# The order of the first four row-major score groups of a head pair, in a one-core attention and feed-forward layer

## The chip, the cores and the metric

One NeuronCore of a Trainium2 chip runs the whole layer. The metric is the device time of one execution in microseconds; the engines are PE (TensorE), DVE (VectorE), ACT (ScalarE), POOL (GpSimd) and SP (SyncE, which issues the transfers).

## The reference

The input x is (8, 1024, 256) in float32. With 16 heads of 16 query and key dimensions and 64 value dimensions:

```python
Q = _split_heads(x, H)
K = _split_heads(x @ Wk + bk, H)
V = _split_heads(x @ Wv + bv, H)
scores = jnp.einsum('bhqd,bhkd->bhqk', Q, K) + mask      # causal
attn = jax.nn.softmax(scores, axis=-1)
o = jnp.einsum('bhqk,bhkd->bhqd', attn, V)
y = x + jax.nn.gelu(o, approximate=False) @ Wf + bf
x = _layernorm(x + y)
x = _layernorm(x + ffn(x))          # silu(x wg) * (x wu), times wd
```

## The kernel before

The program has three parts. A short first part projects keys and values of two units of 512 tokens. The middle part, `attend`, runs 69 steps over 64 pairs of heads (8 batches, 8 pairs each) and takes most of the time. The last part, `finish`, does the output product, the layer norms and the feed-forward product per unit of 512 tokens.

**What a step does.** The scores of a pair are computed twice. In step r, the *row-major* scores of pair r are formed (queries on the partitions), and DVE takes the maximum of each row from them. Two steps later, in step r + 2, the *transposed* scores of the same pair are formed (keys on the partitions) with the maxima already subtracted inside the product, ACT writes their exponentials to `weights`, POOL masks the diagonal blocks and adds the blocks up for the denominators, and PE multiplies them with the values (`weigh`). So in a step, row-major work of pair r stands beside transposed work of pair r - 2. Both come in twelve groups of two heads: s0 to s11 for the row-major groups (listed in `GS` as query tile and key half), t0 to t11 for the transposed ones (`GT`).

**The ring.** Scores go through three two-bank PSUM buffers (`ring`, line 704 is the matmul helper) in the fixed order t0 s0 t1 | s1 t2 s2 | t3 s3 t4 | s4 t5 s5 | t6 s6 t7 | s7 t8 s8 | t9 s9 t10 | s10 t11 s11. Each bar ends one of eight blocks of the step. A buffer comes free for its third successor: PE forms t(j + 2) only when DVE has taken the maximum of s(j) (so t2 waits for s0, t3 for s1, t4 for s2, t5 for s3), and s(j + 1) only when ACT has made the exponential of t(j). PE works strictly in program order, so a group that waits holds back everything behind it, the products with the values too: weigh of t9 and t10 of the pair before follow t1, that of t11 follows s2, those of t0 and t1 follow t4, each at its block's end.

**The maxima on DVE.** A row-major group is 128 queries by up to 512 keys for each of two heads. `top` handles three kinds: a *full* first half (query tiles 4 to 7, key half 0) is one reduction of 128x1024 into `part_max` (line 1109); a group with a causal diagonal is two custom instructions, one for each head, of 128, 256, 384 or 512 columns with the mask added (line 1117, each followed by the read of its accumulator); a second half (key half 1) does the same and takes the stored part maximum in.

**What else DVE does in a step.** In block 1, after s1 and s2, it transposes the shift parts (line 1129). In every fourth step (r divisible by 4, up to 52) it converts the next input unit: the high part after s3 (line 1071), the low part in block 4. In steps 5, 9, ... 53 it adds the bias to keys and splits them *ahead of s0* (lines 1082 and 1086), because the key projection of the step before has ended by then. In blocks 4 and 5 it begins the sum of weights (lines 1138, 1143).

**Projections beside the steps.** Up to step 55, PE also runs two or three projection products (six matmuls of 512 columns each) in a step, one of them at the end of block 1 (behind s2 and the product of t11), the others at the ends of blocks 6 and 7. From step 57 on there are none.

**The loop.** Steps 0 to 11 are written out, steps 12 to 51 are ten rounds of a loop whose body is four steps, and steps 52 to 68 are written out again. So steps 16, 20, ... 48 begin right behind a branch on each engine. The loop's top is at line 76, and the step's shift transposition begins with a register instruction of line 1124.

Of the kernel before, what the change touches and what calls it, by code (L numbers as in the profile page):

```python
# [51 lines left out]
SROWS = 48  # L52
SHROWS = 2
GT = tuple((0, u) for u in range(4)) + tuple((1, u) for u in range(8))
GS = ((0, 0), (4, 0), (5, 0), (2, 0), (6, 0), (7, 0), (1, 0), (4, 1), (5, 1), (3, 0), (6, 1), (7, 1))
NS = 12
NBURST = 8
RINGP = 3
# [24 lines left out]
def settle(eng, passed):  # L83


    eng.sem_inc(passed, 1)
# [7 lines left out]
def build(nc, xT, x, Wk, bk, Wv, bv, Wf, bf, wg, wu, wd, out):  # L94
# [26 lines left out]
    with ExitStack() as ctx:  # L121
# [580 lines left out]
        def _(pe):  # L702
# [54 lines left out]
            def score(j, r, n, it):  # L757

                q, k = Q[r % RING], K[r % RING]
                u, kc = GS[j]  # L760
                w = min(BANK, P * (u + 1) - BANK * kc)
# [285 lines left out]
        def _(dve):  # L1047
# [55 lines left out]
            def top(j, r, n):  # L1103

                u, kc = GS[j]
                w = min(BANK, P * (u + 1) - BANK * kc)
# [5 lines left out]
                if kc == 1:  # L1112

                    dve.wait_ge(s_max, NS * n + GS.index((u, 0)) + 1)
                    settle(dve, s_passed["dve"])
# [200 lines left out]
```

## Time and profile before

| what | value |
|---|---|
| median of 3 runs | 1959.52 us (1958.96 to 1960.97) |
| profiled execution | 1962.14 us, its span 1960.4 us |
| busy share of the span | PE 95%, DVE 73%, POOL 59%, ACT 53% |
| mean granted TensorE clock | 0.976 of full speed |
| steps 36, 37, 38, 39 (start of t0 to start of the next t0) | 23.90, 20.37, 21.46, 19.94 us |
| step 59 and step 60 (no projections) | 19.22 and 20.83 us |

The span is the time from the first to the last instruction of the profiled execution, which is 1.7 us less than its own device time. A step is the unit to think in: 64 of them with row-major work, some 20 us each. A matmul's recorded end is modelled, so the busy share of PE says little about spare time; the starts of successive groups say more.

### The profile page before, as it was taken

How to read it: one execution, taken by the hardware profiler on the slowest of the kernel's cores; microseconds unless marked ns; L12 is line 12 of the kernel's file. 1: busy time of each engine (PE TensorE's matmuls, PEld its weight loads, DVE VectorE, ACT ScalarE, POOL GpSimd, SP SyncE). 2: the span in 40 equal slices, each digit the busy share in tenths (PEclk: the TensorE clock that was granted, in tenths of full speed). 3: DMA queues.
4: the chain of work that ended last, by engine and by line, in shares of the span. 5: the costliest groups of instructions: out<-in, count | busy, mean ns of one | idle time of the engine just before them, and what ended most of it. 6: DMA issues, size and time to landing. Idle time of an engine off the chain costs nothing. (4 is left out here: it accounts for less than half of the span.)

```text
span 1960.4 us, 38648 instructions
## 1 busy us (share of the span) xinstructions
PE 1855.1 (95%) x10304; PEld 961.9 (49%) x10304; DVE 1424.2 (73%) x3469; ACT 1039.1 (53%) x1523; POOL 1158.1 (59%) x1328
## 2 busy tenths in 40 slices
PE   6799999999999999999999999989898999999996
PEld 5344444444444444444444444333255777767773
DVE  3877877777786777778677777767537787887874
ACT  2155555555555555555555556555554564555643
POOL 2187777777768777776877786887832122221222
PEclk9699999999999999999999999999899999999998
DMA  8955556455565545555454664456157667566610
GB/s 267 252 152 158 166 138 185 132 175 158 143 181 132 173 132 174 159 144 182 132 170 131 178 166 142 116 156 151 60 133 181 182 158 190 167 160 180 163 55 22
DMA packets 261008, 303.55 MB, mean 155 GB/s; under 512 B 28048, under 2 KB 177680, under 8 KB 260880
## 3 DMA queue, kind: packets, MB, share of 16 engines
q1 hardware_dynamic: 260880, 302.19, 55.6%
q14 instruction: 90, 0.74, 0.1%
q8 instruction: 38, 0.62, 0.1%
HBM read 174.20 MB, written 127.93 MB: 154 GB/s over the span
## 5 line engine op out<-in xcount | busy, mean ns | idle before, releaser
L964 ACT ACTIVATE weights<-ring 128x1024 f32<-128x1024 f32 (+3 forms) x768 | 599.2, 810 | 332.8 <-PE ring L704 328.1
L672 POOL TENSOR_TENSOR weight_sum<-weight_sum,weights 128x512 f32<-128x512 f32 (+3 forms) x448 | 682.0, 1522 | 9.8
L704 PE MATMUL o_acc<-weights,v_pair 128*64 128x512 f32 (+3 forms) x3072 | 620.1, 510 | 10.8 <-POOL weights L636 6.0
L1109 DVE TENSOR_REDUCE part_max<-ring 128x2 f32<-128x1024 f32 x256 | 301.3, 1218 | 129.4 <-PE ring L704 129.4
L636 POOL TENSOR_SCALAR_AFFINE_SELECT weights<-weights 128x256 f32<-128x256 f32 x512 | 217.6, 430 | 298.1 <-ACT weights L964 297.4
L695 POOL TENSOR_TENSOR h_lo<-hidden,h_hi 128x512 f16<-128x512 f32 x96 | 114.2, 1191 | 391.2 <-ACT h_hi L933 391.2
L704 PE MATMUL ring<-q_stack,k_stack 50*128 50x512 f32 (+3 forms) x1536 | 308.4, 407 | 37.6 <-DVE rowmax L1117 23.0
L1117 DVE CUSTOM_DVE_ANT_0 scrap<-ring,causal 128x128 bf16<-128x128 f32 (+3 forms) x512 | 229.5, 486 | 135.4 <-PE ring L704 132.0
L704 PE MATMUL ring<-k_stack,q_stack 48*128 48x512 f32 (+3 forms) x1536 | 304.2, 399 | 18.0 <-DMA k_stack<-k_rows 8.9
L704 PEld LDWEIGHTS o_acc<-weights,v_pair 128*64 128x64 f32 x3072 | 174.4, 137 | 234.1 <-issue 198.8
L1117 DVE CUSTOM_DVE_ANT_0 scrap<-ring,causal,part_max 128x128 bf16<-128x128 f32 (+3 forms) x512 | 251.1, 546 | 47.6 <-PE ring L704 47.2
L704 PEld LDWEIGHTS ring<-q_stack,k_stack 50*128 50x128 f32 x1536 | 144.9, 186 | 250.9 <-DVE rowmax L1117 114.5
L704 PEld LDWEIGHTS ring<-k_stack,q_stack 48*128 48x128 f32 x1536 | 147.2, 189 | 198.6 <-ACT weights L964 143.0
L704 PE MATMUL ring<-wf_sb,g 128*128 128x256 f32 x1024 | 230.5, 380 | 1.4 <-DVE y_pre L1206 0.8
L704 PEld LDWEIGHTS ring<-wf_sb,g 128*128 128x128 f32 x1024 | 191.4, 190 | 31.6 <-issue 2.2
L933 ACT ACTIVATE v_unit<-o_acc 128x512 f32<-128x512 f32 x112 | 67.0, 599 | 255.2 <-PE o_acc L704 255.2
L1159 DVE TENSOR_TENSOR g<-g,den_wide 128x512 f32<-128x512 f32 x128 | 147.8, 1180 | 8.8 <-DMA g<-o_heads 6.8
L672 POOL TENSOR_TENSOR weight_sum<-weights 128x768 f32<-128x768 f32 x64 | 116.6, 1821 | 0.0
L704 PE MATMUL o_acc<-wv_hi,x_hi 128*128 128x512 f32 x224 | 101.3, 452 | 0.0
L1138 DVE TENSOR_TENSOR weight_sum<-weights 128x1024 f32<-128x1024 f32 x64 | 78.1, 1220 | 18.2 <-PE o_acc L704 18.2
L704 PE MATMUL o_acc<-wv_lo,x_hi 128*128 128x512 f32 x224 | 89.3, 399 | 0.0
L704 PE MATMUL o_acc<-wv_hi,x_lo 128*128 128x512 f32 x224 | 88.7, 396 | 0.0
(105 smaller groups left out, 2057.5 us busy)
## 6 DMA issues: line engine op xcount, KB each, us to landing
v_pairs<-v_unit SPq DMA_DIRECT2D x64, 512.0 KB, 3.5
v_pair<-v_pairs SPq DMA_DIRECT2D x64, 512.0 KB, 5.3
o_heads<-o_pair SPq DMA_DIRECT2D x64, 512.0 KB, 3.5
g<-o_heads SPq DMA_DIRECT2D x16, 2048.0 KB, 8.1
den_wide<-reciprocals SPq DMA_DIRECT2D x32, 1024.0 KB, 13.3
q_stack<-q_rows SPq DMA_DIRECT2D x128, 192.0 KB, 3.7
k_stack<-k_rows SPq DMA_DIRECT2D x128, 192.0 KB, 4.3
q_rows<-x_hi SPq DMA_DIRECT2D x32, 512.0 KB, 3.6
```

What stands on the lines that cost most here:

```text
L636: pool.affine_select(out=diag, in_=diag, compare_op=ALU.is_ge, fill=0.0, base=0, pattern=[[0, 2], [1, P]], channel_multiplier=-1).then_inc ...
L672: pool.tensor_tensor(dst, other, W[t][:, :, :], ALU.add).then_inc(s_add, 1)
L695: pool.tensor_tensor(h_lo[:, f], h32[f % 2][:], h_hi[:, f], ALU.subtract).then_inc(s_hl, 1)
L704: return nc.tensor.matmul(o, l, r, start=start, stop=stop)
L933: return nc.scalar.activation(o, i, ACT.Copy)
L964: nc.scalar.activation(W[t][:, :, :], bank_of("t", t)[:, :, 0:width_of(t)], ACT.Exp).then_inc(s_w, 1)
L1109: v.tensor_reduce(part[r % 2][:, u - 4, :], bank_of("s", j)[:, :, 0:w], AX.X, ALU.max).then_inc(s_max, 1)
L1117: e = v.tensor_tensor_reduce(out=scrap[j % 2][h][:, 0:w], in0=bank_of("s", j)[:, h, 0:w], in1=causal[:, BANK - w:BANK], scale=1.0, scalar= ...
L1138: v.tensor_tensor(acc1[:], W[4][:], W[5][:], ALU.add).then_inc(s_add1, 1)
L1159: v.tensor_tensor(g[r % 2][:, c], g[r % 2][:, c], dn[r % 2][:, c], ALU.mult).then_inc(s_gn, 1)
```

## The change

The table `GS` gives the order in which the row-major groups of a pair are formed by PE and reduced by DVE. The first four entries change places; the other eight stay.

```diff
-GS = ((0, 0), (4, 0), (5, 0), (2, 0), (6, 0), (7, 0), (1, 0), (4, 1), (5, 1), (3, 0), (6, 1), (7, 1))
+GS = ((4, 0), (0, 0), (2, 0), (5, 0), (6, 0), (7, 0), (1, 0), (4, 1), (5, 1), (3, 0), (6, 1), (7, 1))
```

| group | before | after |
|---|---|---|
| s0 | diagonal block of 128 columns | full, 512 columns |
| s1 | full, 512 columns | diagonal block of 128 columns |
| s2 | full, 512 columns | diagonal block of 384 columns |
| s3 | diagonal block of 384 columns | full, 512 columns |

Each group of two heads keeps its work on every engine. The full groups of query tiles 4 and 5 still come ahead of the second halves (s7 and s8) that need them.

## Rows read from the trace of the kernel before

**Rows 1.** The page's head, whole execution

```profile
span 1960.4 us, 38648 instructions
```

**Rows 2.** Groups by line and shape, DVE, 400 to 1240 us: busy, mean, idle

```profile
L1109 DVE TENSOR_REDUCE part_max<-ring 128x2 f32<-128x1024 f32 x159 | 187.2, 1218 | 69.9 <-PE ring L704 69.9
...
L1117 DVE CUSTOM_DVE_ANT_0 scrap<-ring,causal 128x384 bf16<-128x384 f32 x80 | 41.4, 555 | 18.9 <-PE ring L704 18.4
...
L1117 DVE CUSTOM_DVE_ANT_0 scrap<-ring,causal 128x128 bf16<-128x128 f32 x80 | 20.0, 288 | 41.6 <-PE ring L704 39.0 <-issue 2.6
```

**Rows 3.** Timeline of step 37, DVE: start, duration, line, operation, idle before

```profile
831.12 0.75 DVE L1086 SCALAR_TENSOR_TENSOR k_lo<-o_acc,bk_sb,k_hi 128x512 fp32r<-128x512 f32 x1
831.78 0.28 DVE L1117 CUSTOM_DVE_ANT_0 scrap<-ring,causal 128x128 bf16<-128x128 f32 x1
...
832.61 2.36 DVE L1109 TENSOR_REDUCE part_max<-ring 128x2 f32<-128x1024 f32 x2 [0.33 <-PE ring L704]
```

**Rows 4.** Timeline of step 37, PE: t2, then the products of t0 and t1

```profile
832.41 0.32 PE L704 MATMUL ring<-q_stack,k_stack 50*128 50x256 f32 x2
...
835.77 1.72 PE L704 MATMUL o_acc<-weights,v_pair 128*64 128x512 f32 x8
```

**Rows 5.** Timeline of step 38, PE (s0, t2)

```profile
850.40 0.23 PE L704 MATMUL ring<-k_stack,q_stack 48*128 48x128 f32 x2
...
852.34 0.28 PE L704 MATMUL ring<-q_stack,k_stack 50*128 50x256 f32 x2
```

**Rows 6.** Timeline of step 38, DVE (s0)

```profile
850.82 0.29 DVE L1117 CUSTOM_DVE_ANT_0 scrap<-ring,causal 128x128 bf16<-128x128 f32 x1 [0.94 <-PE ring L704]
```

**Rows 7.** Timeline of step 36, behind the loop's branch, DVE

```profile
808.36 0.29 DVE L1117 CUSTOM_DVE_ANT_0 scrap<-ring,causal 128x128 bf16<-128x128 f32 x1 [2.77 <-PE ring L704]
...
812.67 0.21 DVE L1129 STREAM_TRANSPOSE shiftT<-shift_parts 128x32 f32<-128x32 f32 x1 [1.53 <-issue]
...
813.90 1.77 DVE L1071 CAST x_hi<-xt 128x1024 fp32r<-128x1024 f32 x1
815.59 2.34 DVE L1109 TENSOR_REDUCE part_max<-ring 128x2 f32<-128x1024 f32 x2
```

**Rows 8.** Timeline of step 36, PE: t2, t4, t6

```profile
808.93 0.39 PE L704 MATMUL ring<-q_stack,k_stack 50*128 50x256 f32 x2 [0.69 <-DVE rowmax L1117]
...
811.83 0.40 PE L704 MATMUL ring<-q_stack,k_stack 50*128 50x512 f32 x2
...
816.86 0.50 PE L704 MATMUL ring<-q_stack,k_stack 50*128 50x512 f32 x2 [0.16 <-DVE part_max L1109]
```

**Rows 9.** Line 1124 in step 36: DVE's queue (DVEq), register instruction

```profile
L1124 DVEq FUSED_REGOPS  x1: 64/64/64, 812.4 to 812.4; - x1
```

**Rows 10.** DMA queues, 810.3 to 811.3 us: packets, MB, share of 16 engines

```profile
q14 instruction: 1, 0.01, 1.9%
```

**Rows 11.** Timeline of step 61 (no projections), DVE, PE and POOL

```profile
1333.43 0.44 PE L704 MATMUL ring<-q_stack,k_stack 50*128 50x384 f32 x2 [0.69 <-DVE rowmax L1117]
...
1335.58 2.35 DVE L1109 TENSOR_REDUCE part_max<-ring 128x2 f32<-128x1024 f32 x2 [1.78 <-PE ring L704]
...
1336.86 0.33 PE L704 MATMUL ring<-q_stack,k_stack 50*128 50x128 f32 x2 [0.60 <-DVE part_max L1109]
...
1337.34 0.41 POOL L636 TENSOR_SCALAR_AFFINE_SELECT weights<-weights 128x256 f32<-128x256 f32 x1
...
1337.99 0.50 PE L704 MATMUL ring<-q_stack,k_stack 50*128 50x512 f32 x2 [0.58 <-DVE part_max L1109]
...
1338.39 0.77 POOL L636 TENSOR_SCALAR_AFFINE_SELECT weights<-weights 128x256 f32<-128x256 f32 x2
...
1338.42 3.25 PE L704 MATMUL o_acc<-weights,v_pair 128*64 128x512 f32 x8
```

**Rows 12.** Windows of steps 59 and 61: length, busy by engine, PEclk, DMA

```profile
1298.00:1302.00 4.00, 4.00 (x28) 1.47 (x28) 2.36 (x6) 2.54 (x3) 4.00 (x6) 1.00 0.42 92
...
1338.00:1342.00 4.00, 4.00 (x12) 1.31 (x14) 0.98 (x5) 1.51 (x2) 4.00 (x6) 0.57 1.07 217
```

## The prediction

> **What bounds the kernel now.** I read the page first, then DVE's groups by shape, then the timelines of single steps on PE and DVE, since the change moves nothing but the order inside a step. The sum is made against the profiled execution, 1962.14 us with a span of 1960.4 us [rows 1]; that is 2.6 us above the median of the runs, so I add the change of the span to 1959.5 us. Within 0.2% (3.9 us) a measurement of this kernel can't tell a change from none.
>
> No engine has less work or more after the change. What can move is who waits. The price list on DVE: a full group is one reduction of 1.22 us; a diagonal group of 384 columns is two instructions of 0.56 us, one of 128 columns two of 0.29 us [rows 2]. What counts for PE is the time from DVE's start on a group to the matmul that it lets go. For the 128-column group that is 0.57 us (s0 at 808.36, t2 at 808.93), for a full one 1.27 us (s4 at 815.59, t6 at 816.86) [rows 7, 8]. So with s0 full, t2 can come 0.70 us later after the same start of DVE. With s1 at 128 columns, t3 gets free earlier by the same amount, with s2 at 384 columns t4 a little, and t5 waits for a full s3. PE is in program order: whatever t2 loses, the products and projections behind it lose too. The reader is to see in each step whether t2 or t3 and t4 are the ones that wait.
>
> **The five kinds of steps.** Counts come from the loops and conditions in the code.
>
> *Ordinary steps* (29, like step 38). PE forms s0 at 850.40, and DVE starts on it at 850.82, idle until then [rows 5, 6]. A full s0 has 384 more columns, at 2.4 GHz 0.16 us, so DVE would start at 850.98 and let t2 go at 852.25. PE arrives at t2 at 852.34 [rows 5], and that arrival does not move, since s0's extra 0.16 us is what s1 saves. Nothing lost, nothing won; the margin is 0.1 us, so I keep ±0.05 us a step, ±1.5 us in all. The later t1 leaves ACT's exponential on time, because ACT is still on t0's.
>
> *Steps with a key split ahead of s0* (13: steps 5, 9, ... 53). In step 37 DVE comes to s0 only at 831.78, directly behind the key split that starts at 831.12 [rows 3]. Now t2 could go at 831.78 + 0.57 = 832.35 and does go at 832.41 [rows 4]: on the edge. With a full s0 it goes at 831.78 + 1.27 = 833.05, 0.64 us later. Until the products of t0 and t1 at 835.77 [rows 4] PE has 3.36 us filled with s2, a product, a projection and t3, s3, t4, so the loss stays but for a few hundredths. I take 0.62 us (bounds 0.5 and 0.7): 13 x 0.62 = +8.1 us.
>
> *Steps behind the loop's branch* (9: steps 16, 20, ... 48). Here DVE has two gaps that no other engine explains: 2.77 us ahead of s0, and 1.53 us put down to "issue" ahead of the shift transposition [rows 7]. In the second the queue's first instruction of line 1124 runs only at 812.4 [rows 9]: the sequencer had not even reached the waits of the transposition, and a packet of the instruction queue is moved between 810.3 and 811.3 us [rows 10]. I read it as a load of code that begins at a fixed place in the instruction stream, behind the sixth engine instruction after the branch: two for each head of s0 (a maximum and a read), and the reductions of s1 and s2. After the change the first six are s0's one, s1's four, and then already s2's first. If the place stays, the gap opens in front of s2's pair, and s2, which t4 waits for, is done only after it. In numbers: DVE resumes at 812.4 to 812.65, s2 takes 2 x 0.5 us, the transposition 0.3 us with its wait, and the full s3 1.2 us, so the conversion of x begins at 814.85 to 815.2 us instead of 813.90 [rows 7], 0.95 to 1.3 us later. t4, now at 811.83 [rows 8], goes at about 813.5 to 813.8. From the conversion on DVE has no idle time up to s4 at 815.59, and PE waits for it at t6 [rows 7, 8], so the delay of DVE is the delay of the step. I take 1.15 us: 9 x 1.15 = +10.4 us. The lower bound is the gap staying where it is: then only s3's 1.22 us against 0.96 us (a 384 group with its reads) remains, 0.25 us, +2.3 us; the upper one is 1.4 us, +12.6 us.
>
> The Trainium skill, Advanced Engine Details and Errata, says under ISA Cache that an engine holds two blocks of 256 instructions (TensorE more); that would make the gap a load at a fixed place, as I read the rows. Its Control Flow Timing gives about 108 ns for a compare-and-branch; by that price alone, with no load, there would be neither of the two gaps, the trace with 2.77 us disagrees, and the sum would be 8 us lower.
>
> *Written-out steps with the conversion of x* (4: steps 4, 8, 12, 52). No gap there, but the conversion follows s3 and DVE is late afterwards in the same way: 4 x 0.27 = +1.1 us (0 to 1.5).
>
> *Steps without projections* (7: steps 57 to 63). This is where the old order hurts. In step 61 t1 waits 0.69 us for the last group of the pair before, t3 waits 0.60 us and t4 0.58 us for the reductions of s1 and s2, which begin at 1335.58 [rows 11]. After the change s0 is done long before t2 comes; s1 and s2 free t3 some 0.85 us and t4 some 0.95 us earlier, about 1337.05. But then POOL is late next: the product of t0 needs the masked block, whose select begins at 1337.34 and lasts 0.41 us, and that of t1 the first of the two that begin at 1338.39 together for 0.77 us [rows 11]. The first product could start at 1337.8 instead of 1338.42, the second at 1338.82 instead of 1338.42 + 0.86 = 1339.28 at full clock. So 0.46 us is won; POOL's own chain up to there runs from the block t8 of the step before and doesn't move against it. I take 0.43: 7 x 0.43 = -3.0 us (bounds -2.0 and -6.6, the latter if POOL moves along).
>
> **The clock.** In step 61 the products of t0 and t1 take 3.25 us [rows 11], in step 37 1.72 us [rows 4]. The granted clock is 0.57 in that stretch, and 1.00 in the same stretch of step 59 [rows 12]: part of the window at 1.2 GHz, the rest at 2.4. Of the seven such steps five are like 61. What PE did before: three waits of 0.6 to 0.7 us in some 5 us [rows 11]. Steps 36 to 38 with one wait or none and a projection keep the full clock. The change takes two of the three waits away and puts one of about 0.4 us in front of the product; I take it that the clock then stays: 5 x (3.25 - 1.72) = -7.7 us, with 0 as the other bound. Behind the branch the reverse can happen: t2's wait of 0.69 us [rows 8] becomes 1.2 us, and at t4 there is a new one. A fall of the clock there is partly hidden by that second wait. I take +1 us in all, bounds 0 and +8.
>
> **Sum.** 8.1 + 10.4 + 1.1 - 3.0 - 7.7 + 1.0 = +9.9 us on the span: 1969.4 us.
>
> **Rivals.**
>
> *The gap stays at the transposition.* If what DVE waits for there is a matter of time or of the transposition and not of a place in the stream, the steps behind the branch lose 0.25 us by DVE. t2's later start is then uncovered, and a falling clock costs more, say 4 us. 8.1 + 2.3 + 1.1 - 3.0 - 7.7 + 4 = +4.8 us, 1964.3 us. Against it: the packet of instructions in just that time [rows 10]. Chance 0.20.
>
> *The clock still falls in the last seven steps.* A wait for POOL replaces the two for DVE, and PE may still have too little to do. Then -7.7 us is missing: 1977 us. Chance 0.20.
>
> *Faster: the later t2 costs nothing.* If something behind it, in the steps with a key split and behind the branch, sets the products of t0 and t1 anyway (ACT's copy of the projection is the candidate), the losses vanish and the gains of the last steps stay: -3.0 - 7.7, 1949 us, and some 1952 with a part of the losses. It decides from 0.62 us of PE idle between t2 and those products in step 37; I find at most 0.1 us there. Chance 0.05.
>
> *No change.* The losses and the gains are each smaller and cancel, or the ring hides both: 1959.5 us. Chance 0.08.
>
> *Worse than the sum.* The clock falls behind the branch in most of the nine steps, at 1.5 us each, with no cover: 1982 us. Chance 0.05.
>
> **The numbers.** The forecast has 0.42. The range reaches from 1962 to 1980 us; it leaves out the faster case, the unchanged one and the worst, 0.18. Slower by more than 0.2% (above 1963.4 us): the forecast, the falling clock, the worst case and 0.6 of the first rival, 0.79. Within 0.2%: the unchanged case and the rest of that rival, 0.16. Faster: 0.05.
>
> **What the profile after would show.** Step 37: t2 some 0.64 us later against the key split, and a step of about 21.0 us. Step 36: the "issue" gap in front of the custom pair of 384 columns and no longer in front of the transposition, t4 held by it, the step near 25 us. Step 38: unchanged. Steps 57 to 63: t3 and t4 without their waits for DVE, the product of t0 waiting for POOL, granted clock 1.00. The prediction is wrong if the gap behind the branch does not move, if the low clock stays at the end, or if ordinary steps lose the 0.1 us of margin that I count on: 29 of them at 0.1 us are 3 us.

## Result and profile after

The changed kernel takes 1974.44 us (median of 4, 1971.93 to 1975.59) against 1959.53 us before: ratio 1.0071, 95% interval 1.0055 to 1.0087, so it is slower, by 14.9 us. The forecast was 1969.4 us, +9.9, in a range of 1962 to 1980. The profiled execution is the fastest of the four, 1971.93 us with a span of 1970.2 us, 9.8 us over [rows 1]. That this is so near the forecast of +9.9 is luck in part: the profiled execution of the kernel before, 1962.14 us, is 2.6 us above the median of that kernel's runs, and this one is 2.5 us below the median of its own. The other three are 1.9 to 3.7 us longer, with a mean granted clock of 0.976 to 0.977 where the profiled one has 0.980.

I took the length of each step, from its t0 to the next one's, in both traces, and added the differences by kind of step:

| steps | forecast, us | profile after, us |
|---|---|---|
| 13 with a key split ahead of s0 | +8.1 | +8.5 (0.62 to 0.68 each) |
| 9 behind the branch | +10.4 and +1.0 for the clock | +14.1 (seven of them 0.93 to 1.49, step 44 1.68, step 48 3.70) |
| 4 written out, with conversion of x | +1.1 | -0.3 |
| 7 last ones | -3.0 - 7.7 | -8.6 |
| the other 28 steps from 3 to 56 | 0 | -1.5 (0.05 each) |
| start up to the end of step 2, and step 64 | 0 | +1.1 and -1.7 |

That is +11.7 us; the rest of the span's +9.8 lies in the last part, 1.9 us shorter. The rows with a forecast of 0 miss by -4.0 us together with the last part, and hide that the others came out 3.8 us higher than forecast. In two of them the clock can be read: the mean granted clock of step 2 is 0.92 where it was 0.99, that of step 64 is 0.91 where it was 0.83. The change gives no reason for either.

Timeline of the changed kernel, DVE, step 36 (t0 at 817.20), which answers to [rows 7]: start, duration, operation, idle before.

```profile
819.63 1.23 DVE L1109 TENSOR_REDUCE part_max<-ring 128x2 f32<-128x1024 f32 x1 [2.66 <-PE ring L704]
820.78 0.28 DVE L1117 CUSTOM_DVE_ANT_0 scrap<-ring,causal 128x128 bf16<-128x128 f32 x1
820.98 0.28 DVE L1117 CUSTOM_DVE_ANT_0 scrap<-ring,causal 128x128 bf16<-128x128 f32 x1
823.90 0.56 DVE L1117 CUSTOM_DVE_ANT_0 scrap<-ring,causal 128x384 bf16<-128x384 f32 x1 [2.62 <-issue]
824.38 0.55 DVE L1117 CUSTOM_DVE_ANT_0 scrap<-ring,causal 128x384 bf16<-128x384 f32 x1
824.86 0.21 DVE L1129 STREAM_TRANSPOSE shiftT<-shift_parts 128x32 f32<-128x32 f32 x1
825.24 1.23 DVE L1109 TENSOR_REDUCE part_max<-ring 128x2 f32<-128x1024 f32 x1 [0.17 <-PE ring L704]
826.38 1.23 DVE L1071 CAST x_hi<-xt 128x1024 fp32r<-128x1024 f32 x1
```

The "issue" gap has left the transposition and stands in front of s2's pair, as the prediction had put it. It ends 6.70 us after t0; before, the transposition ran 6.88 us after t0 (812.67 against 805.79) [rows 7]. On PE, t2 starts 3.71 us after t0 (3.14 before) and t4 7.80 us after it (6.04 before) [rows 8].

```profile
820.91 0.39 PE L704 MATMUL ring<-q_stack,k_stack 50*128 50x256 f32 x2 [1.31 <-DVE part_max L1109]
...
825.00 0.80 PE L704 MATMUL ring<-q_stack,k_stack 50*128 50x512 f32 x2
```

Step 37 (t0 at 842.48), DVE and PE: the full s0 follows the key split directly, and t2 starts 3.38 us after t0 instead of 2.72 us [rows 3, 4].

```profile
843.93 0.75 DVE L1086 SCALAR_TENSOR_TENSOR k_lo<-o_acc,bk_sb,k_hi 128x512 fp32r<-128x512 f32 x1
844.60 1.21 DVE L1109 TENSOR_REDUCE part_max<-ring 128x2 f32<-128x1024 f32 x1
...
845.86 0.39 PE L704 MATMUL ring<-q_stack,k_stack 50*128 50x256 f32 x2 [0.65 <-DVE part_max L1109]
```

Step 61 (t0 at 1349.56), which answers to [rows 11]: t3 no longer waits, t4 waits 0.34 us, and then the products wait for POOL's select.

```profile
1353.50 0.33 PE L704 MATMUL ring<-q_stack,k_stack 50*128 50x128 f32 x2
...
1354.45 0.50 PE L704 MATMUL ring<-q_stack,k_stack 50*128 50x512 f32 x2 [0.34 <-DVE rowmax L1117]
...
1354.79 0.41 POOL L636 TENSOR_SCALAR_AFFINE_SELECT weights<-weights 128x256 f32<-128x256 f32 x1
...
1355.34 1.92 PE L704 MATMUL o_acc<-weights,v_pair 128*64 128x512 f32 x8 [0.38 <-POOL weights L636]
```

The granted clock in the window of those products is 1.00 (the third figure from the end of the row below, with the columns of [rows 12]), and they take 1.92 us instead of 3.25. The opposite happens in step 48, behind the branch: the same products take 3.25 us there, after t2 had waited 1.27 us and t4 0.33 us. The mean granted clock from 1086 to 1094 us is 0.63.

```profile
1354.00:1358.00 4.00, 3.28 (x18) 1.13 (x16) 1.98 (x5) 1.79 (x4) 3.82 (x8) 1.00 1.01 231
```

```profile
1083.28 0.39 PE L704 MATMUL ring<-q_stack,k_stack 50*128 50x256 f32 x2 [1.27 <-DVE part_max L1109]
...
1087.51 0.79 PE L704 MATMUL ring<-q_stack,k_stack 50*128 50x512 f32 x2 [0.33 <-DVE rowmax L1117]
1088.23 3.25 PE L704 MATMUL o_acc<-weights,v_pair 128*64 128x512 f32 x8
```

### The profile page after: what moved, and what is told of

Same layout as the page of the kernel before. It is cut to its first block and busy times, and to the rows that moved or that the text cites. A ratio compares the mean times of both kernels' runs of the same rounds, so it can differ in the third digit from the quotient of the medians.

```text
span 1970.2 us, 38648 instructions
## 1 busy us (share of the span) xinstructions
PE 1855.0 (94%) x10304; PEld 961.3 (49%) x10304; DVE 1426.0 (72%) x3469; ACT 1039.6 (53%) x1523; POOL 1162.8 (59%) x1328
## 5 line engine op out<-in xcount | busy, mean ns | idle before, releaser
L1109 DVE TENSOR_REDUCE part_max<-ring 128x2 f32<-128x1024 f32 x256 | 306.6, 1219 | 193.7 <-PE ring L704 181.2
L704 PE MATMUL ring<-q_stack,k_stack 50*128 50x512 f32 (+3 forms) x1536 | 314.7, 409 | 47.5 <-DVE rowmax L1117 23.2
```

The source lines that it names most:

```text
L704: return nc.tensor.matmul(o, l, r, start=start, stop=stop)
L1109: v.tensor_reduce(part[r % 2][:, u - 4, :], bank_of("s", j)[:, :, 0:w], AX.X, ALU.max).then_inc(s_max, 1)
```

## Experiments

Twelve kernels were run, in three groups of four, each group beside its own runs of the kernel before (medians 1959.22, 1959.89 and 1958.64 us); the ratios are against these. NEW is the order of the change, and N is a number of idle instructions, told below. Differences by steps are those of the profiled executions against [rows 1].

### One kind of step at a time

```diff
+def order_of(r):
+    return GS_NEW if <condition> else GS
...
-                u, kc = GS[j]
+                u, kc = order_of(r)[j]
```

**Condition `r % 4 == 1`.**

> The new order only in steps 1, 5, 9, ... of each four (in row-major work; 13 of them have a key split ahead of s0), the old one elsewhere. Theory (t2 waits for a full s0 that DVE begins late): steps 5, 9, ... 53 longer by 0.64 us each, steps 57 and 61 shorter by 0.3 to 1.9 us, all others as before; 1965 to 1968 us. Rival (the cost of the change is spread over all steps or sits in the ordinary ones): these steps gain less than 0.3 us each, 1960 to 1963 us.

Measured: 1966.58 us, ratio 1.0043 (1.0027 to 1.0060). By steps: +8.6 us in the 13, 0.63 to 0.70 us each, as the theory has it to 0.06 us a step, and +1.0 in the nine behind the branch although their order is the old one. Steps 57 and 61, which have the new order, are 1.9 us shorter; of the five old ones beside them two are 1.6 us shorter and one 1.6 us longer, as the clock falls in other steps than before.

**Condition `r % 4 == 0 and 12 <= r < 52`.**

> The new order only in steps 12, 16, ... 48 (nine of them behind the loop's branch), the old one elsewhere. Theory (the code load opens inside s2): each of the nine longer by 1.3 us, and more where the granted clock falls behind it; step 12, with no branch before it, unchanged; 1971 to 1976 us, and the widest spread of the four kernels of this call. Rival (only s0's later release of t2 counts): 0.6 us each, 1965 us.

Measured: 1981.17 us (1973.09 to 1988.48), ratio 1.0114 (1.0088 to 1.0140). Seven of the nine steps take 24.7 to 25.2 us, two 26.8 and 27.1; step 12 is unchanged, and the 13 split steps differ by -0.03 us in all. By the steps the theory is right and the rival wrong; the median is 5 us above the theory's range, and the spread is the widest of the four, 15 us. It goes with the clock: 1973.09 to 1976.35 us in three runs at a mean granted clock of 0.972 to 0.976, 1985.99 to 1988.48 in the three others at 0.964 to 0.967. The windows of the two long steps, 44 and 48, show 0.57:

```profile
990.00:998.00 8.00, 8.00 (x30) 3.41 (x28) 4.38 (x8) 2.83 (x5) 5.38 (x7) 0.57 0.26 78
1079.00:1087.00 8.00, 7.82 (x28) 2.96 (x26) 4.19 (x8) 2.96 (x5) 5.01 (x6) 0.57 0.29 84
```

**Condition `r >= 57`.**

> The new order only in steps 57 to 63. Theory: steps 57 to 63 shorter by 0.3 us each and by 1.9 us where the old order let the clock fall, all others as before: 1949 to 1952 us. Rival (the gain at the end needs the shifted steps before it, by where they put the clock's falls): 1956 to 1959 us.

Measured: 1951.34 us (1947.26 to 1955.46), ratio 0.9960 (0.9946 to 0.9974). The last seven steps alone are worth 8 us by the medians (10.1 us in the profiled execution, the fastest of its six); no help from the steps before them is needed.

The medians of the three pieces do not add up to the change: +7.4, +22.0 and -7.9 us make +21.5, where the whole change costs 14.9. In the traces the pieces agree with the whole kind by kind, but for how often the clock falls. Behind the branch it falls in steps 16, 24, 44 and 48 with only these steps changed, in 36 and 48 in the whole change. That the rest of the 6.6 us is more falls in the runs without a trace is likely from their clocks, but not shown.

### Where the gap behind the branch sits

**Only s0 and s1 changed** (`GS = ((4, 0), (0, 0), (5, 0), (2, 0), ...`).

> Order full, 128, full, 384: only s0 and s1 change places against before. Theory (the load of code sits behind the tenth instruction after the branch, which is s2's reduction again): the gap is back in front of the shift transposition, and the nine steps lose 0.2 us instead of 1.3; split steps +0.64 us each, last steps as in the full change (-8.5 us): 1958 to 1963 us. Rival (the branch steps lose because s0 is full, whatever s2 is): the nine steps lose 1.3 us each as in the full change, 1970 to 1975 us.

Measured: 1970.33 us (1967.53 to 1971.21), ratio 1.0052 (1.0038 to 1.0067): the time misses the theory's range by 7 us and lies just inside the rival's. The place of the gap is the theory's, back in front of the transposition:

```profile
822.34 1.23 DVE L1109 TENSOR_REDUCE part_max<-ring 128x2 f32<-128x1024 f32 x1 [0.30 <-PE ring L704]
825.04 0.21 DVE L1129 STREAM_TRANSPOSE shiftT<-shift_parts 128x32 f32<-128x32 f32 x1 [1.48 <-issue]
```

Three of the nine steps (24, 32, 40) take 25.14 to 25.22 us and the other six 23.7 to 24.05; the clock falls in just these three. The nine together lose 6.3 us where the theory had 1.8 and the rival 11.7, so neither has the size. The split steps lose 0.68 to 0.74 us each (+9.3). What the theory had left out is t2's wait: it is 1.03 to 1.32 us in these nine steps, 0.49 to 0.83 us before, and with it the clock falls in some of them though s2 is full.

**The code moved, the order left.** N increments by DVE of a semaphore that nobody waits for stand ahead of its first step, and move all the code behind them, the loop too:

```diff
+            for _ in range(N):
+                settle(dve, s_passed["dve"])
             walk(dve, *LOOP_B, attend)
```

N = 12, order of before:

> The kernel before with twelve semaphore increments of DVE ahead of its step loop, which move its code in the instruction stream. Theory (a load of code at a fixed place, ten instructions behind the loop's top): the place is now ahead of the loop's top, the 1.53 us gap of the steps 16, 20, ... is gone or far from there, the 2.77 us gap behind the branch stays; the nine steps 0.5 to 1.5 us shorter, 1946 to 1955 us. Rival (the gap belongs to the transposition or to a time): nothing moves, 1959 to 1960 us.

N = 12, order NEW:

> The changed kernel with the same twelve increments. Theory: the 2.6 us gap in front of s2's pair is gone, the nine steps lose only what t2's later release costs (0 to 0.6 us against before), 1952 to 1962 us. Rival (gap tied to the operation or to a time): as the changed kernel, 1972 to 1976 us.

N = 4, order of before:

> The kernel before with four such increments. Theory (fixed place): the load comes four instructions earlier, in front of s1's or between s0's and s1's reductions, so the gap moves from the transposition to there, s1 and with it t3 is late by about 2 us; steps behind the branch 0 to 1 us longer than before, 1959 to 1968 us. Rival (tied to the transposition): nothing moves.

N = 9 and N = 10, order of before:

> The kernel before with nine increments: one instruction short of where the loop's top reaches the fixed place. Theory (blocks of code at fixed places; the loop's body is held whole only if it touches one block fewer): the gap opens behind the first record of the step, in front of s0, and ends 6.6 us after t0 as in all kernels so far; t2 waits until 7.3 us, the nine steps are 4 to 5 us longer, 1995 to 2005 us, with 103 instruction packets on the queue. Rival (what helped in the shift by twelve was something else, gradual in the number): between the shift by four and the shift by twelve.

> The kernel before with ten increments, one more than the other. Theory: the loop's top stands at the start of a block, all loads in the loop vanish, 58 instruction packets, the nine steps 1.0 us shorter each: 1950 to 1955 us, some 45 us from the kernel that differs by one increment. Rival: as the shift by nine.

| kernel | time, us | ratio (95%) | steps 16, 20, ... 48, us each | where the gap stands |
|---|---|---|---|---|
| before, N = 4 | 2001.82 | 1.0213 (1.0197 to 1.0228) | 27.7 to 29.2 | ahead of s1, 3.70 us |
| before, N = 9 | 2016.24 | 1.0287 (1.0273 to 1.0301) | 29.0 to 30.3 | ahead of s0, 6.85 us |
| before, N = 10 | 1952.05 | 0.9963 (0.9950 to 0.9976) | 22.7 | none |
| before, N = 12 | 1953.07 | 0.9965 (0.9954 to 0.9977) | 22.7 | none |
| after, N = 12 | 1951.30 | 0.9960 (0.9943 to 0.9976) | 22.6 to 22.7 | none |

One idle instruction more or less, N = 9 or N = 10, is 64 us. The second gap stands where it was expected with N = 4 and 9, and is gone with 10 and 12. Expected wrongly for N = 12 was that the 2.77 us ahead of s0 would stay: that gap is gone too, in both orders, and the changed kernel with N = 12 is 0.7 us faster than the range given for it. With N = 4 and N = 9 the times lie 34 us and 11 us above their ranges. For N = 4 I had the load end earlier because its place comes earlier; for both I had left out the clock, which falls in all nine of these steps in either trace. DVE in step 36 with N = 4 and with N = 9, the record before the gap and the one behind it:

```profile
832.61 0.08 DVE L1117 DVE_READ_ACCUMULATOR2_ANT rowmax<- 128x1 f32 x1
836.39 2.35 DVE L1109 TENSOR_REDUCE part_max<-ring 128x2 f32<-128x1024 f32 x2 [3.70 <-issue]
```

```profile
835.84 0.08 DVE L1117 DVE_READ_ACCUMULATOR2_ANT rowmax<- 128x1 f32 x1
842.77 0.29 DVE L1117 CUSTOM_DVE_ANT_0 scrap<-ring,causal 128x128 bf16<-128x128 f32 x1 [6.85 <-issue]
```

and with N = 10, the same start of a step with both gaps of [rows 7] gone (what is left ahead of s0 is a wait for PE):

```profile
803.37 0.29 DVE L1117 CUSTOM_DVE_ANT_0 scrap<-ring,causal 128x128 bf16<-128x128 f32 x1 [0.94 <-PE ring L704]
...
807.37 0.20 DVE L1129 STREAM_TRANSPOSE shiftT<-shift_parts 128x32 f32<-128x32 f32 x1
```

The gap moves towards the loop's top by exactly the number of instructions that were put ahead. DVE's records from the loop's top to the gap, those of its sequencer counted, are 10 before (s0 6, s1 2, s2 2), 10 after (2, 6, and s2's first 2), 10 with only s0 and s1 changed, 6 with N = 4, and 1 with N = 9. Its end hardly moves: the next record of DVE or its sequencer starts 6.5 to 6.7 us after t0 in step 36 of each of them (with N = 4, DVE at 836.39 against t0 at 829.71; with N = 9, at 842.77 against 836.11), and 6.0 to 6.9 us after t0 over all nine steps. So the earlier the place, the longer the gap. And the packets of the instruction queue say what it is. Queues from 500 to 1180 us, in the kernel before, and then with N = 10:

```profile
q14 instruction: 39, 0.32, 0.2%
```

```profile
q14 instruction: 3, 0.02, 0.0%
```

Over the whole span the pages count 90 packets before and 91 after the change, 45 with N = 10 or 12 (the 103 and 58 of the expectations count those outside the span too). That is 45 fewer, five for each of nine branches back, and ahead of s0 nothing is loaded any more either. DVE's loop body is 296 recorded instructions.

The Trainium skill, Advanced Engine Details and Errata, ISA Cache, gives two blocks of 256 instructions for an engine like this one. By that the loop of the kernel before, its top ten instructions ahead of a block's end, reaches into three blocks (10 + 256 + 30), one too many, and from N = 10 on into two. The step from N = 9 (a gap behind the first record) to N = 10 (none) agrees with it to the instruction; the length of 256 itself no run here tests.

### The pieces put together

Order NEW in steps 57 to 63 only, and N = 12:

> The old order up to step 56, the new one in steps 57 to 63, and the twelve increments: the two gains together. If they add, 1937 to 1946 us, faster than both kernels. Rival (they don't add, as the clock's falls move): 1947 to 1955 us.

Measured: 1942.23 us (1938.44 to 1945.03), ratio 0.9910 (0.9894 to 0.9926). The two gains add: 17.7 us under the kernel before, against 6.8 and 7.9 us by themselves. It is the fastest median here, 32 us under the changed kernel.

Order NEW in all steps but 1, 5, ... 53, with N = 12 and without:

> The new order in all steps but 1, 5, ... 53, the old one in these, and twelve increments. The theory adds: shift -9 us, last steps -8.6 us, 0.05 us in each ordinary step, no loss in the split steps: 1938 to 1944 us, equal to or just below the version with the new order in the last steps alone. Rival (mixing orders costs something at each change of order): 1945 us and more.

> The same without the increments: the changed kernel with the old order back in steps 1, 5, ... 53. Theory: the changed kernel less 13 x 0.65 us: 1964 to 1968 us. Rival (the loss of the split steps turns up elsewhere when it is taken away there): 1970 us and more.

Measured: 1943.05 us (1941.92 to 1943.73), ratio 0.9915 (0.9902 to 0.9929), and 1967.00 us (1960.84 to 1972.27), ratio 1.0033 (1.0020 to 1.0046). In both, the 13 split steps are as before within 0.2 us in all, so their loss is theirs alone. The ordinary steps give 1.3 us, less than the runs differ, and the version with the increments can't be told apart from the one above. Neither rival holds: the first kernel is inside the theory's range, and so is the second. The one without the increments shows again what the steps behind the branch do: in its profiled execution of 1972.27 us four of the nine take 26.8 to 27.1 us, with windows at 0.57 like the ones shown, and the others 24.7 to 25.2; a run of 1961.52 us has a mean clock of 0.979 where that one has 0.973.

## Why the prediction came out as it did

The mechanism held kind by kind, with one exception (the conversion steps). The time came out inside the range, 5.0 us above the forecast. By the steps of the profiled execution the terms missed by +0.4 (split), +2.7 (branch and its clock), -1.4 (conversion), +2.1 (last steps), -1.5 (ordinary) and -2.5 us (what was not in the sum), which nearly cancel. The 5.0 us are, to 0.1 us, the distances of the two profiled executions from their medians, 2.6 and 2.5 us, and no trace says in which steps these lie.

**Split steps.** Right as worked out: 0.62 us taken, 0.65 measured with the rest and 0.66 alone.

**Steps behind the branch.** The place was right, and the 1.15 us nearly: seven of the nine lost 0.93 to 1.49 us, and the eight without step 48 lost 1.29 us in the mean (in one of them, step 36, a fall of the clock lies under the gap: t4 has 0.80 us there instead of 0.40). The first rival (the gap stays at the transposition) is out, by the profile after and by N = 4. Three things were wrong or missing. I had counted the place as behind the sixth engine instruction, which would be between the two heads of s2; only five stand ahead of it after the change. What stays the same is ten records with those of the sequencer counted. I took the load to begin when the sequencer arrives at the place; its end stays at 6.0 to 6.9 us after t0 instead, wherever the place is, so the change never moved the load's end, it only put s2 behind it. And I took the 2.77 us ahead of s0 as given by the branch; it is a load too, gone with N = 10. All of the loss in these steps hangs on the loads: with N = 12 the new order takes 22.64 us there, the old one 22.68.

**The clock behind the branch**, +1 us, is a term that was too small. In the profiled execution it cost some 2.4 us (step 48 against the other eight). The three other runs are 1.9 to 3.7 us longer at a lower mean clock, and the kernel with only these steps changed spreads over 15 us. That the slower runs of one kernel have the lower mean clocks is measured; in which steps of a run without a trace the clock fell, and so how much of the 5.0 us is this term, stays open. The cause of the single fall is open as well: t2 waits 1.07 to 1.37 us in all nine steps after the change, and the clock falls in two of them.

**Conversion steps**, +1.1 us, did not lose anything (-0.06 to -0.09 each). I had s3's 1.22 us begin where its 0.96 us began. But the transposition is done earlier, because s1 and s2 are shorter together and are not late, and s3 starts as soon as PE has it: in step 8, 5.37 us after t0 against 5.51, and the conversion 6.51 against 6.47. The 0.27 us a step was the one overlap that the prediction had wrong.

**Last steps.** Mechanism right, with POOL late next as foreseen: 0.26 to 0.33 us where the clock had been full before (0.43 taken), 1.9 us in four of the five where it had been low (0.43 + 1.53). In the fifth, step 58, the clock fell again and only 0.44 us was won, which is 1.5 of the 2.1 us that are missing. So the second rival (the clock still falls) holds for one step of seven here. Over all traces the clock falls in five or six of these seven steps with the old order (six traces) and in none to two with the new one (seven traces, one of them with only s0 and s1 changed). Why is not shown: the prediction had two of three waits go, but in step 61 only t3's is gone. t1 still waits 0.53 us, t4 0.34 and the products 0.38; before, the three were 0.69, 0.60 and 0.58 us. And before the change steps 59 and 63 had the same three waits as step 61 and kept the clock.

**Ordinary steps** kept their 0.1 us of margin and won 0.05 us each.

The faster rival is out: t2 comes 0.66 us later in step 37, and the step is 0.67 us longer. The unchanged one is out by the interval, and so is the worst case (1982 us).

## What to carry to other kernels

When two shapes change places in a ring that several engines share, go through the kinds of steps one by one: the same order cost 0.65 us where DVE came late to s0 and won 0.05 to 1.9 us where it didn't, and the better kernel uses each where it pays. The gaps behind this loop's branch that no semaphore explains, with packets on the instruction queue beside them, were code loads. When you see such gaps, count the instructions from the loop's top to the gap, and try to move the loop by a few idle instructions before tuning anything inside it. Measure each number: 10 won 7 us here, and 4 and 9 cost 42 and 58 us. And ask of each new wait not only how long it is but whether the granted clock falls behind it.

## What the runs showed of the hardware

A loop body of 296 recorded DVE instructions runs without a stall for code (N = 10, 45 packets on the instruction queue) or with two stalls a round (N = 9, 90 packets), depending on where its top lies: 22.7 us against 29.0 to 30.3 us for the same step, one instruction apart. The second stall ends 6.0 to 6.9 us after t0 in the traces with N = 0, 4 and 9 and in both orders, wherever it begins.

TensorE's granted clock halves for a few us in five of seven steps where no wait is longer than 0.7 us but three follow each other (before, the last steps), and in two of nine with a wait of 1.07 to 1.37 us at t2 (after, steps 36 and 48; in step 48 the products take 3.25 us instead of 1.72). Executions of one program differ in their mean granted clock and their time together: 0.973 at 1972.27 us and 0.981 at 1960.84 us, the ends of twelve runs.
